# Expert bias in a mixture-of-experts stage: two 128-column transposes and eight products in four row parts of TensorE

## The chip, the cores and the metric

The kernel runs on one core of a Trainium2 chip. The metric is device time in microseconds, the median of several executions. One further execution was recorded by the hardware profiler; all rows below are from it. Matmuls run on TensorE (PE), their weight loads are listed as PEld, VectorE is DVE, ScalarE is ACT, GpSimd is POOL, and SyncE (SP) issues the DMAs.

## What is computed

The program is one transformer-like layer on 8 sequences of 1024 tokens of width 256. A first phase (a selective state-space scan with its projections, then residual and layer norm) gives `x1`. The second phase adds attention with 16 heads of 16 columns and a mixture of 8 experts, and ends in a layer norm:

```
gate = softmax(x @ W_gate + b_gate)                    # 8 values a token
combine = gate at its two largest values, 0 elsewhere
expert_out = einsum("bsd,edf->bsef", x, W_experts) + b_experts
moe_out = einsum("bsef,bse->bsf", expert_out, combine)
return layernorm(x + attn_out + moe_out)
```

The change touches one part of `moe_out`: the bias. Summed over experts it is `combine @ b_experts`, for each tile of 128 tokens a product of a 128x8 with an 8x256 matrix, in fp32.

## The kernel before

The first phase ends at about 1887 us of the span and is not touched. The second one, `attention_phase`, takes the batches b = 0 to 7 one after another: an expert stage (`experts`) and then the heads (`heads`). Each engine has its own instruction list, written by hand, and waits on semaphores; what stands behind a waiting instruction waits too.

In the expert stage the 1024 tokens are 8 tiles t, and a unit u = 4t + e2 is the product of one tile with two experts, six fp16 matmuls of 512 columns (L1419) into one PSUM bank. PSUM has 8 banks; `EBANK[u]` says which one a unit uses, and `used(b, v)` makes TensorE wait until the earlier unit v of the bank was read. DVE weighs the even units and adds them up in `acc` (L1753, L1756, L1764). ACT weighs the odd ones into `scaled` (L1561), and POOL adds those to `x_in` (L1241). DVE's `join` (L1700) adds the two sums of a tile. From unit 13 on, TensorE puts the first scores of the heads in between (L1261), and DVE takes their row maxima (L1628). From batch 1 on DVE also does the layer norm of the batch before (L1674, L1679).

The weights `comb` (128 tokens x 8 tiles x 8 experts) are made by DVE. Behind the units of tile 1 TensorE waits until banks 0 and 1 are free (`used(b, 4)`, `used(b, 5)`) and turns `comb` tile by tile (L1437), ACT copies the result out to `combT` (L1566), and behind the units of tile 2 TensorE forms the eight products with `b_e` (L1445):

```
for q in range(TT):
    mm = pe.transpose(ps[0:E, q // 4, ...], comb[:, q, :], ident[:, :])
...
for q in range(TT):
    mm = pe.matmul(ps[:, q // 2, (q % 2) * H:(q % 2 + 1) * H], combT[:, q * P:(q + 1) * P],
                   b_e[:, :], start=True, stop=True)
```

DVE adds them to the sums in five additions (L1782): three of two tiles, two of one.

The heads start once POOL has done its last addition; there ACT takes the exponentials (L1503), TensorE the scores (L1300, L1261) and the products of the probabilities with v (L1313, four column parts of 32), whose sums it turns back (L1328).

Before the first batch the phase is set up: SP loads weights (L1138 to L1148), POOL clears and fills tiles (L1215 to L1227), DVE and ACT scale the weights. `WEIGHTS` is the count that the engines wait for on the loads.

## Time and profile before

| | us |
|---|---|
| median of 3 runs (3902.52 to 3905.53) | 3902.99 |
| the profiled execution | 3907.31 |
| its span, from the first to the last instruction | 3905.5 |
| busy in the span: PE / DVE / ACT / POOL | 3588.3 / 3426.8 / 2617.0 / 1667.7 |
| mean granted TensorE clock, share of full speed | 0.954 |

In the rows a time is in microseconds from the span's start, and a form as 128x512 is partitions times elements. In a timeline a row gives start, length, engine, line, operation, `out<-in` with the tiles' names, the form and the count of instructions merged in it. In brackets stands how long the engine had been idle before, and which instruction ended that. `combT` is a piece of the tile `probs` and appears under that name. "issue" means that nothing that the profile shows was waited for. An fp32 matmul that isn't a transpose leaves two records.

### The profile page before, as it was taken

Reading aid. Unit: us, or ns where it says so; the run is one execution under the profiler, and the core shown is the slowest. Engines: PE = TensorE matmul, PEld = TensorE weight load, DVE = VectorE, ACT = ScalarE, POOL = GpSimd, SP = SyncE. Lnnn points to the kernel's source line nnn. Section 1 sums busy time; section 2 is a strip of 40 time slices with the busy share of each in tenths; the row PEclk is TensorE's granted clock in tenths of the full one; section 3 lists DMA queues with packets and bytes.
Section 4 is the critical chain, followed back from the end, with each engine's and each line's share of the span. In section 5 each row is a group of like instructions: output and inputs, shape, how many; then the busy total and the mean of one; then the engine's idle time right before and its main releaser. Section 6 shows DMA issues by size and latency. Waiting matters only on the chain.

```text
span 3905.5 us, 121218 instructions
## 1 busy us (share of the span) xinstructions
PE 3588.3 (92%) x52170; PEld 1623.6 (42%) x52170; DVE 3426.8 (88%) x3617; ACT 2617.0 (67%) x3895; POOL 1667.7 (43%) x1054
## 2 busy tenths in 40 slices
PE   5989989899998989898389999999999999999997
PEld 3545455454545545454232423324233242332422
DVE  5898999989999999988689798897988979889796
ACT  4655657665664766655149588595885958869588
POOL 4777778777777777777320110201102011020200
PEclk8999999899999999999699999999999999999999
DMA  3543434444443444443160601506015060240500
GB/s 96 134 116 105 137 100 126 110 132 116 111 137 100 126 121 130 110 102 105 65 86 2 85 26 25 85 2 87 23 27 83 2 87 23 33 78 2 87 12 12
DMA packets 145113, 307.59 MB, mean 79 GB/s; under 512 B 24456, under 2 KB 64016, under 8 KB 144336
## 3 DMA queue, kind: packets, MB, share of 16 engines
q1 hardware_dynamic: 144592, 299.94, 34.0%
q8 instruction: 412, 6.75, 0.7%
q14 instruction: 109, 0.89, 0.1%
HBM read 230.66 MB, written 35.13 MB: 68 GB/s over the span
## 4 chain that ended last, share of the span: by engine, by line
PE 23%; ACT 11%; issue 9%; DVE 7%; POOL 0%; DMA 0%; ACTq 0%; SPq 0%; DVEq 0%; POOLq 0%
ACT probs L1503 9%; PE ps L1313 6%; PE ps L1300 5%; PE ps L1419 4%; DVE neg_max L1628 3%; PE ps L1348 2%; PE ps L1261 2%; PE ps L1328 1%; PE ps L1361 1%; ACT o_sb L1510 1%; PE ps L1445 1%; DVE acc L1764 1%; ACT m_rows L1516 1%; DVE diag_b L1786 1%; DVE x1T L1594 1%
## 5 line engine op out<-in xcount | busy, mean ns | idle before, releaser
L350 POOL TENSOR_TENSOR z<-z,c_rep 128x1024 f32<-128x1024 f32 x512 | 1357.2, 2666 | 457.4 <-DVE z L864 451.7
L1503 ACT ACTIVATE probs<-ps,e_scale 128x512 f32<-128x512 f32 x2048 | 1241.8, 688 | 132.9 <-PE ps L1300 117.8
L864 DVE TENSOR_TENSOR_SCAN z<-dA,ps 128x1024 f32<-128x1024 f32 x512 | 1150.9, 2273 | 130.7 <-PE ps L408 76.2
L1628 DVE TENSOR_REDUCE neg_max<-ps 128x1 f32<-128x1024 f32 x1024 | 1204.2, 1218 | 45.5 <-PE ps L1261 41.1
L705 ACT ACTIVATE dA<-rep,a_rep 128x1024 f32<-128x1024 f32 x512 | 574.3, 1144 | 332.0 <-DVE z L864 327.6
L408 PEld LDWEIGHTS ps<-diag,u_t 64*64 64x64 f32 x32768 | 544.0, 139 | 424.5 <-issue 424.3
L408 PE MATMUL ps<-diag,u_t 64*64 64x64 f32 x32768 | 606.8, 225 | 107.3 <-DVE z L864 84.0
L1300 PE MATMUL ps<-q_st,k_st 50*128 50x512 f16 x2048 | 676.5, 393 | 29.9 <-ACT probs L1503 17.6
L1313 PE MATMUL ps<-probs,v_h 128*32 128x256 f32 x8192 | 658.0, 396 | 0.6 <-ACT o_sb L1510 0.6
L1247 POOL COPY v_h<-v_all 128x80 f32 (+1 forms) x256 | 62.0, 244 | 1283.0 <-PE ps L1313 1283.0
L1261 PE MATMUL ps<-k_st,q_st 48*128 48x512 f16 x2048 | 581.1, 393 | 3.6 <-DVE neg_max L1628 3.5
L427 PE MATMUL ps<-z,eye 128*64 128x512 f32 x2048 | 512.8, 622 | 3.8 <-POOL z L350 2.7
L1241 POOL TENSOR_TENSOR x_in<-x_in,probs 128x256 f32<-128x256 f32 x256 | 191.3, 747 | 417.4 <-ACT probs L1561 405.5
L1419 PE MATMUL ps<-w_e,x1T 128*128 128x512 f16 x1536 | 359.1, 388 | 8.7 <-DVE acc L1764 8.7
L1300 PEld LDWEIGHTS ps<-q_st,k_st 50*128 50x128 f16 x2048 | 159.5, 94 | 467.9 <-ACT probs L1503 240.6
L1313 PEld LDWEIGHTS ps<-probs,v_h 128*32 128x32 f32 x8192 | 168.5, 108 | 361.6 <-issue 181.3
L1561 ACT ACTIVATE probs<-ps,comb_s 128x256 f32<-128x256 f32 x256 | 106.3, 470 | 258.8 <-PE ps L1419 203.9
L427 PEld LDWEIGHTS ps<-z,eye 128*64 128x64 f32 x2048 | 127.4, 139 | 250.8 <-issue 222.9
L1419 PEld LDWEIGHTS ps<-w_e,x1T 128*128 128x128 f16 x1536 | 146.3, 99 | 201.4 <-DVE acc L1764 25.2
L1261 PEld LDWEIGHTS ps<-k_st,q_st 48*128 48x128 f16 x2048 | 133.7, 93 | 60.7 <-issue 25.8
L439 PE MATMUL ps<-w_io,s_res 128*128 128x256 f32 x576 | 139.3, 392 | 1.3 <-DVE s_res L845 1.3
L619 ACT ACTIVATE u_t<-ps 128x1024 f32<-128x1024 f32 x32 | 32.6, 1018 | 146.3 <-PE ps L382 146.3
(189 smaller groups left out, 3283.6 us busy)
## 6 DMA issues: line engine op xcount, KB each, us to landing
c_rep<-c_scratch SPq DMA_DIRECT2D x512, 256.0 KB, 4.0
rep<-delta SPq DMA_DIRECT2D x128, 256.0 KB, 5.0
q_st<-qk_halves SPq DMA_DIRECT2D x192, 128.0 KB, 10.0
k_st<-qk_halves SPq DMA_DIRECT2D x192, 128.0 KB, 10.7
qk_halves<-qk_parts SPq DMA_DIRECT2D x32, 512.0 KB, 11.0
x_nat<-in_x SPq DMA_DIRECT2D x9, 1024.0 KB, 9.7
x_rows<-x_nat SPq DMA_DIRECT2D x9, 1024.0 KB, 6.8
xT<-in_xT SPq DMA_DIRECT2D x8, 1024.0 KB, 7.4
```

Source lines behind the costliest of these rows:

```text
L350: pool.tensor_tensor(z[:, k % ZR, :], z[:, k % ZR, :], c_rep[:, slot, :], ALU.mult).then_inc(s_zc, 1)
L408: mm = pe.matmul(ps[q * QD:(q + 1) * QD, 2 + 2 * (k % 2) + r, i * TB:(i + 1) * TB], u_t[rows, i, m * P + j * QD:m * P + (j + 1) * QD], dia ...
L427: mm = pe.matmul(ps[j * QD:(j + 1) * QD, half, :], eye[:, :], z[:, (grp * QN + j) % ZR, half * HALF:(half + 1) * HALF], start=False, stop= ...
L705: act.activation(dA[:, k % AR, :], rep[:, slot, :], ACT.Exp, scale=a_rep[:, m, j, g:g + 1]).then_inc(s_da, 1)
L864: dve.tensor_tensor_scan(z[:, k % ZR, :], dA[:, k % AR, :], pair(1 + k % 2), 0.0, ALU.mult, ALU.add).then_inc(s_z, 1)
L1241: pool.tensor_tensor(to, to, scaled[:, i % 2, e, :], ALU.add).then_inc(s_pa, 1)
L1261: mm = pe.matmul(ps[:, 2 * (qt % 2) + half, :], head(q_st, half, QR, h, qt * P, P), head(k_st, half, QR, h, half * HALF, HALF), start=True ...
L1300: pe.matmul(ps[:, ring_bank(("probs", h, 2 * kt + half)), :], head(k_st, half, QM, h, kt * P, P), head(q_st, half, QM, h, half * HALF, HAL ...
L1313: mm = pe.matmul(ps[VC * j:VC * (j + 1), 6, 0:n], v_h[:, kt, :], probs[:, kt, j * n:(j + 1) * n], start=(kt == 0), stop=(kt == TT - 1), sk ...
L1419: mm = pe.matmul(ps[:, EBANK[u], :], x1T[:, x, k, t * P:(t + 1) * P], w_e[:, w, k, e2 * 2 * H:(e2 + 1) * 2 * H], start=(i == 0), stop=(i = ...
L1503: act.activation(probs[:, kt, half * HALF:(half + 1) * HALF], ps[:, ring_bank(("probs", h, 2 * kt + half)), :], ACT.Exp, scale=e_scale[:, ...
L1628: dve.tensor_reduce(neg_max[:, qt:qt + 1], pair(qt % 2), AX.X, ALU.max, negate=True).then_inc(s_mx, 1)
```

## The change

`comb` is now laid out with 32 columns a tile (`comb_wide`, 128 x 8 x 32, cleared once on POOL), of which the first 8 hold the weights. So four tiles are 128 columns, and TensorE turns them in one transpose: two instead of eight, both into bank 0. In the result, the weights of tile 4i + j lie in partitions 32j to 32j + 7 and columns 128i to 128i + 127. ACT's copy is 128x256 instead of 8x1024. The table of biases is loaded four times, to partitions 32j to 32j + 7 (three DMAs more, `WEIGHTS` from 16 x 5 to 16 x 8). Each product reads its 8 rows at partition 32j, so four in a row use four different row parts of the array, and they write to four banks, j, at columns 256i. DVE's additions read two neighbouring banks at the same columns instead of 512 columns of one bank. No instruction changes its place in any engine's list; POOL has one more at the start, SP three.

```diff
-        b_e = sb("b_e", [E, H])
+        b_e = sb("b_e", [P, H])
...
-        comb = sb("comb", [P, TT, E])
+        comb_wide = sb("comb", [P, TT, VC])
+        comb = comb_wide[:, :, 0:E]
...
-        combT = probs[0:E, 1, :]
+        combT = probs[:, 1, 0:2 * P]
...
-        WEIGHTS = 16 * 5
+        WEIGHTS = 16 * 8
...
-            for dst, src in ((b_e, d["b_e"]), (b_vg, d["b_vg"].broadcast_to([P, GV]))):
-                sp.dma_start(dst[:, :], src).then_inc(s_w, 16)
+            for j in range(QUARTERS):
+                sp.dma_start(b_e[j * VC:j * VC + E, :], d["b_e"]).then_inc(s_w, 16)
+            sp.dma_start(b_vg[:, :], d["b_vg"].broadcast_to([P, GV])).then_inc(s_w, 16)
...
+            pool.memset(comb_wide[:, :, :], 0.0)
             pool.memset(b_one[:, :], 0.0).then_inc(s_const, 1)
...
-                        for q in range(TT):
-                            mm = pe.transpose(ps[0:E, q // 4, (q % 4) * P:(q % 4 + 1) * P], comb[:, q, :], ident[:, :])
+                        for i in range(2):
+                            mm = pe.transpose(ps[:, 0, i * P:(i + 1) * P],
+                                              comb_wide[:, i * QUARTERS:(i + 1) * QUARTERS, :].rearrange("p j e -> p (j e)"), ident[:, :])
                         mm.then_inc(s_cbt, 1)
...
-                        for q in range(TT):
-                            mm = pe.matmul(ps[:, q // 2, (q % 2) * H:(q % 2 + 1) * H], combT[:, q * P:(q + 1) * P],
-                                           b_e[:, :], start=True, stop=True)
+                        for i in range(2):
+                            for j in range(QUARTERS):
+                                rows = slice(j * VC, j * VC + E)
+                                mm = pe.matmul(ps[:, j, i * H:(i + 1) * H], combT[rows, i * P:(i + 1) * P],
+                                               b_e[rows, :], start=True, stop=True)
                         mm.then_inc(s_eb, 1)
...
-                        act.activation(combT, pair(0)[0:E, :], ACT.Copy).then_inc(s_cbe, 1)
+                        act.activation(combT, ps[:, 0, 0:2 * P], ACT.Copy).then_inc(s_cbe, 1)
...
-                            to = to[:, first:last, :].rearrange("p t h -> p (t h)")
-                            bias = ps[:, first // 2, (first % 2) * H:(first % 2 + last - first) * H]
+                            to = to[:, first:last, :]
+                            i, j = first // QUARTERS, first % QUARTERS
+                            bias = ps[:, j:j + last - first, i * H:(i + 1) * H]
                             dve.tensor_tensor(to, to, bias, ALU.add).then_inc(s_eba, 1)
```

## Rows read from the trace of the kernel before

**Rows 1.** The chain that ended last, 2200 to 2280 us (start, length, what)

```profile
2224.36 3.65 PE ps L1445 x16
...
2233.90 1.21 DVE neg_max L1628
```

**Rows 2.** Waits of DVE, 1968 to 3720 us (total, times, longest)

```profile
DVE x_in L1782 <- PE ps L1445: 24.1, 8, 3.4
```

**Rows 3.** Timeline of DVE, expert stage of batch 1

```profile
2223.11 0.48 DVE L1756 SCALAR_TENSOR_TENSOR acc<-ps,comb_s,acc 128x256 f32<-128x256 f32 x1 [0.65 <-PE ps L1419]
...
2224.69 0.41 DVE L1700 TENSOR_TENSOR acc<-acc,x_in 128x256 f32<-128x256 f32 x1
2228.05 1.62 DVE L1782 TENSOR_TENSOR x_in<-x_in,ps 128x512 f32<-128x512 f32 x3 [2.95 <-PE ps L1445]
...
2232.76 2.35 DVE L1628 TENSOR_REDUCE neg_max<-ps 128x1 f32<-128x1024 f32 x2 [0.65 <-PE ps L1261]
```

**Rows 4.** Timeline of PE, the same stretch

```profile
2218.15 1.03 PE L1437 MATMUL ps<-ident,comb 128*8 128x128 f32 x8 [0.87 <-issue]
2219.02 5.34 PE L1419 MATMUL ps<-w_e,x1T 128*128 128x512 f16 x24
2224.30 3.72 PE L1445 MATMUL ps<-b_e,probs 8*128 8x256 f32 x16
2227.94 4.45 PE L1419 MATMUL ps<-w_e,x1T 128*128 128x512 f16 x12
2232.33 0.60 PE L1261 MATMUL ps<-k_st,q_st 48*128 48x512 f16 x4
```

**Rows 5.** Timelines of DVE and of PE, batch 0, at the bias products

```profile
1988.57 1.62 DVE L1782 TENSOR_TENSOR x_in<-x_in,ps 128x512 f32<-128x512 f32 x3 [3.43 <-PE ps L1445]
...
1988.46 2.76 PE L1419 MATMUL ps<-w_e,x1T 128*128 128x512 f16 x12
```

**Rows 6.** Line 1445 alone (ns), then timeline of PE: products of v, 128-column transposes

```profile
L1445 PE MATMUL ps<-b_e,probs x128: 374/374/478, 1984.8 to 3681.3; 8*128 8x256 f32 x128
...
2169.14 0.64 PE L1313 MATMUL ps<-probs,v_h 128*32 128x256 f32 x8
...
2198.84 2.37 PE L1313 MATMUL ps<-probs,v_h 128*32 128x256 f32 x40
...
2203.84 0.38 PE L1328 MATMUL ps<-ident,o_sb 128*128 128x128 f32 x2
2204.06 2.86 PE L1361 MATMUL ps<-w_vg,x1T 128*128 128x264 f16 x24
```

**Rows 7.** Stretches: window, us, busy us of each engine, then PEclk

```profile
2228.70:2232.10 3.40, 3.40 (x10) 1.07 (x8) 3.37 (x8) 0.00 (x0) 0.00 (x0) 0.50 1.07 125
```

**Rows 8.** Timeline of ACT, batch 1; line 1510 alone (min/median/max ns)

```profile
2219.22 1.02 ACT L1566 ACTIVATE probs<-ps 8x1024 f32<-8x1024 f32 x1 [0.58 <-PE ps L1437]
...
L1510 ACT ACTIVATE o_sb<-ps x128: 382/383/433, 2040.5 to 3884.4; 128x256 f32<-128x256 f32 x128
```

**Rows 9.** Timeline of the set-up, 1884 to 1918 us

```profile
1887.89 0.21 POOL L1215 MEMSET ones<- 128x128 f32 x1 [35.84 <-POOLq L91]
...
1890.88 0.51 SPq L1147 DMA_DIRECT2D b_e<-in_b_e  x1
...
1896.59 20.39 DVE L1786 TENSOR_SCALAR diag_b<-ident,b_qk 128x128 f32<-128x128 f32 x4
1903.05 13.78 POOL L1223 MEMSET k_st<- 32x16384 f16 x1
```

**Rows 10.** Timeline of ACT, first and last exponentials of heads, batches 2 and 3

```profile
2507.91 1.26 ACT L1503 ACTIVATE probs<-ps,e_scale 128x512 f32<-128x512 f32 x2 [1.71 <-POOL x_in L1241]
...
2683.01 1.26 ACT L1503 ACTIVATE probs<-ps,e_scale 128x512 f32<-128x512 f32 x2
...
2751.16 1.26 ACT L1503 ACTIVATE probs<-ps,e_scale 128x512 f32<-128x512 f32 x2 [1.71 <-POOL x_in L1241]
...
2925.45 1.26 ACT L1503 ACTIVATE probs<-ps,e_scale 128x512 f32<-128x512 f32 x2
```

## The prediction

> **What bounds the kernel now.** I read the page first, then the chain that ended last around one batch's expert stage, then the waits of VectorE, then the two engines in order of time. The page's busy shares decide little, for they are averages over stages with different limits, and a matmul's end is modelled. The chain says more. In batch 1 it runs through TensorE up to and through the bias products, and a few microseconds later it passes to VectorE [rows 1], which works almost without a gap until the heads begin. So what ends latest in the expert stage is VectorE's work, as far as TensorE lets it start. The waits say when it does not: 24.1 us in 8 waits for the bias products alone [rows 2].
>
> In batch 1 VectorE stands still three times [rows 3]: 0.65 us for expert unit 10, 2.95 us for the bias products, 0.65 us for the first scores after them. Together 4.25 us. TensorE's side of the same stretch [rows 4]: eight transposes take 0.87 us from their start to the next group's (2218.15 to 2219.02), sixteen records of bias products last 3.72 us (eight fp32 matmuls, two records each). The twelve expert matmuls behind them need 4.45 us, where the same twelve in batch 0 need 2.76 [rows 5]. In batch 0 the wait for the bias is 3.43 us and there is no third one [rows 5]; the other seven then have (24.1 - 3.4) / 7 = 2.95 us each.
>
> **Transposes.** Eight matmuls of 8 columns become two of 128. Two transposes of 128 columns stand in the trace already: they start at 2203.84 and the next matmul at 2204.06 [rows 6], 0.22 us. Saved on TensorE: 0.87 - 0.22 = 0.65 us. Their start does not move: by the code they wait for VectorE's unit 4, and TensorE stood idle 0.87 us before them [rows 4]. The 0.65 us reaches VectorE whole, since unit 10 is what it waits for, for 0.65 us. At the worst the heavier weight load eats 0.1 us; that is the end of the bound.
>
> **Bias products.** Still eight fp32 matmuls of 256 columns and sixteen records, but each set of four stands in four row parts of the array and in four PSUM banks. Before, all sixteen used the same part, one every (3.72 - 0.48) / 15 = 0.216 us (the last one lasts 0.374, the first 0.478 [rows 6]). Row parts of 32 don't occur in this trace. The nearest row is the products of v, four column parts of 32, also fp32 with 256 columns and two records each: one set of eight records lasts 0.64 us and five sets 2.37 us [rows 6], so a set costs (2.37 - 0.64) / 4 = 0.43 us, twice 0.216: four records share one slot. With that the sixteen records take four slots: 3.72 - 12 x 0.216 = 1.13 us. Bounds: 1.13 us if four run together, 1.99 us if two do (eight slots), 3.72 us if none do. I take 1.13, as in the nearest row. The Trainium skill (TensorE: Matmul & The Clock Gate, Part 3, measured speedup) gives 3.07 times for four row parts instead of my 3.29, which would be 1.21 us and 0.6 us less gain over the eight batches; no row here shows row parts of 32.
>
> **Batch 1 with both.** The products start at 2224.30 - 0.65 = 2223.65 and end at 2224.78; VectorE took 0.03 us after the end, so it goes on at 2224.82 instead of 2228.05, 3.23 us earlier. It arrives there at 2225.10 - 0.65 = 2224.45, so 0.37 us of the wait stay.
>
> **The third wait.** VectorE is ready for the scores at 2232.11 - 3.23 = 2228.88 [rows 3]. TensorE begins unit 12 at 2227.94 - 3.23 = 2224.71. What it then needs depends on its clock. The granted clock was 0.50, the lower of the two levels, from 2228.7 to 2232.1, right after 3.7 us in which TensorE used only 8 rows [rows 7]; batch 0 had the same products and kept its speed, 2.76 us for the twelve [rows 5]. With 1.1 us of such products between dense fp16 matmuls I expect no fall. Scores begun at 2232.33 let VectorE go on at 2232.76, 0.43 us later, and at full clock the twelve matmuls take 2.76 us. Then the scores are there at 2224.71 + 2.76 + 0.43 = 2227.90, a microsecond before VectorE, and the third wait goes: 0.65 us. If the clock still falls, the twelve matmuls take 2232.33 - 2227.94 = 4.39 us, the scores come at 2229.53, and 0.65 us of this wait stays.
>
> Sum of a batch from 1 to 7: 3.23 + 0.65 = 3.88 us, seven times 27.2 us. Batch 0 has the first two terms alone: 3.2 us. After that VectorE has no idle time left in the stage that matters, so any further lead of TensorE is worth nothing: it waits for VectorE to free its banks.
>
> **ACT.** Its copy shrinks from 8x1024 at 1.02 us to 128x256, which costs 0.38 us elsewhere [rows 8]. Worth nothing: the copy ended at 2220.24, its reader starts 4 us later. If it were late, it would cost what the products start later.
>
> **DVE's five additions.** Same elements, but two banks are read in one instruction with a step. I take no change. Bound: the first three, two of two tiles and one of one, took 1.62 us, and a single join 0.41 us [rows 3], so a two-tile addition is about 0.6 us and two single ones 0.82. If each fell apart, that is 0.2 us for each of three, 0.65 us a batch, 5 us in all.
>
> **Set-up.** One memset of 128x256 is added on POOL ahead of two of 13.8 us. VectorE's first four small products took 20.39 us and ended at 1916.98, when POOL's last large memset had ended at 1916.83 [rows 9]: it was held up by them. So POOL's order is on the path here, and the new memset costs its own time. 128x128 took 0.21 us, so I take 0.4 us for twice that (0.2 to 0.6). Three more small loads on SP's queue delay the last two by 3 x 0.5 us; POOL needs them at 1917, 25 us after their issue. Nothing; 1.5 us if that cover went.
>
> **Heads.** Their stage is led by ScalarE, starts when POOL has finished the stage before and moves as a whole. Its length depends a little on where low-clock stretches fall: 176.36 us in batch 2, 175.55 us in batch 3 [rows 10]. I take nothing for it and 0.8 us for seven batches as bound, 5.6 us either way.
>
> **Sum.** -27.2 - 3.2 + 0.4 = -30.0 us. The profiled execution took 3907.31 us (span 3905.5) and would take 3877.3; it stands 4.3 us above the median of the three runs, 3902.99 us, and against that the forecast is **3873.0 us**. Its own range: 5.6 us lower through the heads; higher by 4.6 for a clock that falls still, by 5 for the additions, or by 5.6 through the heads, of which hardly more than 8 come together: 3867 to 3881.
>
> **Rivals.**
> Two at a time. The two records of one fp32 matmul stand behind each other in one row part; if the array keeps program order strictly, only neighbours overlap. Then the products take 1.99 us, 0.86 us more in eight batches: -23 us, 3880 us. Against it: the products of v have the same structure and don't show it.
> No overlap at all. Row parts take turns; only the transposes' 0.65 us is left, eight times, less 0.4: about -5 us, 3898 us, within what can be told apart. For it: no row part of 32 with all 128 columns occurs.
> Clock falls anyway, as the transposes of 128 columns or the products still leave a thin stretch: the third wait stays, -30.0 + 7 x 0.65 = -25.5 us, 3877.5 us. For it: in all batches from 1 on it fell before.
> Slower: a drain between row parts. If the array had to be empty before it takes another part, each record would cost its full 0.374 to 0.478 us [rows 6] instead of 0.216: 16 x 0.43 = 6.9 us, 3.2 us more than now. Less the transposes' 0.65, that is 2.5 us in eight batches, +20 us, 3923 us. It decides from 0.26 us a record upwards, where the products lose what the transposes gave. Against it: four column parts started within one slot, 0.43 us for eight records.
> The change is what it says: the two transposes and eight products stand where the eight and eight stood.
>
> **Numbers.** This effect is measurable from about 0.2% (7.8 us). Forecast 0.75; clock falls anyway 0.08; two at a time 0.08; no overlap 0.05; slower 0.04. Range with the first three and their bounds: 3866 to 3881 us. Faster by over 0.2%: 0.91; within: 0.05; slower: 0.04.
>
> **What would show it.** Bias products: sixteen records within about 1.1 us (2.0 and 3.7 for the rivals, 7 for the slower one). VectorE's waits for them together below 5 us instead of 24.1. Transposes to next matmul 0.22 us. Twelve expert matmuls after the products at 2.76 us and a granted clock of 1.00 there. From the first bias addition to the first exponential of the heads 0.65 us less than before in batches 1 to 7. Set-up later by 0.4 us. The forecast is wrong if VectorE shows a new wait between the additions and the heads, or if the heads get longer by over 1 us a batch.

## The result and the profile after

| | before | changed |
|---|---|---|
| median of 6 runs, us | 3905.27 | 3876.31 |
| lowest to highest, us | 3902.52 to 3919.65 | 3873.27 to 3882.33 |
| ratio, 95% interval | | 0.992 (0.9903 to 0.9938) |
| span of the profiled execution, us | 3905.5 | 3880.5 |

The forecast was 3873.0, range 3866 to 3881. The runs of one kernel differ by 9 to 17 us here, and the profiled executions show where most of it lies: in the first phase, which no edit touches. Over the executions below the second phase starts anywhere from 1870.6 to 1890.2 us of the span. So I compare the second phase alone, and split it at three instructions of each batch that stand in the rows: the first expert matmul of TensorE, VectorE's first bias addition, ScalarE's first exponential.

| us | before | changed | forecast of the difference | measured |
|---|---|---|---|---|
| set-up, to the first expert matmul | 80.41 | 80.61 | +0.4 | +0.2 |
| first expert matmul to first bias addition, batch 0 | 20.26 | 17.07 | -3.2 | -3.2 |
| the same, each of batches 1 to 7 | 21.29 | 18.38 | -3.23, seven times | -2.91, seven times |
| first bias addition to first exponential, batches 1 to 7 | 37.9 (38.57 in batch 3) | 38.04 (38.68 and 38.75 in batches 4 and 7) | -0.65, seven times | +1.6 in all |
| first exponential to the next expert matmul, 8 batches | 1466.3 | 1462.0 | 0, bound 5.6 | -4.3 |
| second phase | 2017.6 | 1991.7 | -30.0 | -25.9 |

The timeline of TensorE in batch 1 of the changed kernel, beside [rows 4]:

```profile
2217.29 0.41 PE L1440 MATMUL ps<-ident,comb 128*128 128x128 f32 x2 [0.87 <-issue]
2217.54 5.60 PE L1422 MATMUL ps<-w_e,x1T 128*128 128x512 f16 x24
2223.07 1.15 PE L1451 MATMUL ps<-b_e,probs 8*128 8x256 f32 x16
2224.14 2.76 PE L1422 MATMUL ps<-w_e,x1T 128*128 128x512 f16 x12
2226.93 0.61 PE L1264 MATMUL ps<-k_st,q_st 48*128 48x512 f16 x4
```

The products last 1.15 us for 3.72, and the twelve matmuls behind them 2.76 for 4.45. The transposes still begin after an idle 0.87 us, and the next group starts 0.25 us behind them (before: 0.87). But the 24 matmuls up to the products take 5.53 us from start to start where they took 5.28: TensorE stands 0.25 us more in them, because it now comes too early for a bank that VectorE still reads (unit 11 goes into the bank of unit 8). This is where 0.25 us of the transposes' gain stayed.

The stretches right behind the products, beside [rows 7] (window, us, busy us of each engine, granted clock):

```profile
2223.07:2226.90 3.83, 3.83 (x29) 1.82 (x29) 3.25 (x8) 0.84 (x2) 1.46 (x2) 1.00 1.07 113
2226.90:2230.00 3.10, 3.08 (x17) 1.23 (x16) 3.06 (x5) 0.84 (x2) 1.45 (x2) 1.00 1.04 120
```

The granted clock stays at 1.00, the upper of its two levels. VectorE in the same batch, beside [rows 3]:

```profile
2223.29 0.41 DVE L1706 TENSOR_TENSOR acc<-acc,x_in 128x256 f32<-128x256 f32 x1
2224.28 1.62 DVE L1789 TENSOR_TENSOR x_in<-x_in,ps 128x512 f32<-128x512 f32 x3 [0.58 <-PE ps L1451]
2225.81 1.01 DVE L1789 TENSOR_TENSOR acc<-acc,ps 128x256 f32<-128x256 f32 x2
...
2228.26 2.35 DVE L1634 TENSOR_REDUCE neg_max<-ps 128x1 f32<-128x1024 f32 x2
...
2234.84 0.69 DVE L82 SCALAR_TENSOR_TENSOR ln<-ln 128x8 f32<-128x8 f32 x1
...
2235.68 0.93 DVE L1706 TENSOR_TENSOR acc<-acc,x_in 128x256 f32<-128x256 f32 x1
```

The wait for unit 10 is gone, 0.58 us of the wait for the products is left, the additions take what they took, and the row maxima start with no wait. Its waits over the whole phase, beside [rows 2]:

```profile
DVE x_in L1789 <- PE ps L1451: 4.9, 8, 0.9
```

So far all is as forecast, within 0.35 us a batch. The last two rows of VectorE's timeline are not. In the kernel before the same two instructions stood like this (VectorE, then POOL, same batch):

```profile
2239.41 0.17 DVE L82 SCALAR_TENSOR_TENSOR ln<-ln 128x8 f32<-128x8 f32 x1
...
2239.72 0.42 DVE L1700 TENSOR_TENSOR acc<-acc,x_in 128x256 f32<-128x256 f32 x1
...
2236.66 1.53 POOL L1241 TENSOR_TENSOR x_in<-x_in,probs 128x256 f32<-128x256 f32 x2 [1.62 <-ACT probs L1561]
2239.89 1.64 POOL L1241 TENSOR_TENSOR x_in<-x_in,probs 128x256 f32<-128x256 f32 x2 [1.71 <-ACT probs L1561]
```

and POOL in the changed kernel:

```profile
2234.78 1.54 POOL L1244 TENSOR_TENSOR x_in<-x_in,probs 128x256 f32<-128x256 f32 x2 [1.99 <-ACT probs L1567]
```

Before, the small layer-norm step and the join began in a gap of POOL. Now POOL starts two additions 0.06 us ahead of the step, and the step takes 0.69 us instead of 0.17 and the join 0.93 instead of 0.42, in all seven batches: 1.03 us. This coincidence is a candidate for where the third wait's 0.65 us went. Counted from the first bias addition, VectorE is 0.80 us ahead of the kernel before when the step begins and 0.23 us behind it after the join. Two later joins, 0.54 and 0.78 us long before, take 0.42 and 0.72 now, which leaves the 0.11 us of the table.

The chain that ended last passes from the products to the additions, as in [rows 1], and then stays with VectorE:

```profile
2223.14 1.12 PE ps L1451 x16
2224.49 0.40 issue
2224.88 1.01 DVE x_in L1789 x2
```

Set-up and ACT's copy, beside [rows 8, 9] (POOL, SP's queue, VectorE, ACT):

```profile
1889.08 0.32 POOL L1220 MEMSET comb<- 128x256 f32 x1
...
1892.01 1.44 SPq L1148 DMA_DIRECT2D b_e<-in_b_e  x4
...
1897.78 20.43 DVE L1793 TENSOR_SCALAR diag_b<-ident,b_qk 128x128 f32<-128x128 f32 x4
...
2217.74 0.39 ACT L1572 ACTIVATE probs<-ps 128x256 f32<-128x256 f32 x1
```

The new memset costs its 0.25 us: from the first memset of the phase to the first large one 1.61 us (1.36 before). The whole set-up took 80.35 to 80.74 us in the ten executions with this set-up, and 80.41 and 80.87 in the two with that of before, so the +0.2 of the table isn't told apart from scatter.

Ahead of unit 19 TensorE now stands 1.99 to 2.00 us for VectorE in each of batches 1 to 7 (0.4 us before, 1.2 in batch 3). In five of them the clock stays up, as in batch 1, and in batches 4 and 7 it falls there (TensorE's timeline in batch 1, then in batch 4, then the stretch):

```profile
2237.57 2.76 PE L1422 MATMUL ps<-w_e,x1T 128*128 128x512 f16 x12 [1.99 <-DVE acc L1770]
...
2953.44 4.36 PE L1422 MATMUL ps<-w_e,x1T 128*128 128x512 f16 x12 [2.00 <-DVE acc L1770]
...
2953.30:2956.70 3.40, 3.26 (x8) 1.16 (x9) 3.29 (x6) 0.80 (x4) 0.00 (x0) 0.50 1.06 123
```

The heads' exponentials, first and last of batches 2 and 3, beside [rows 10]:

```profile
2500.62 0.69 ACT L1509 ACTIVATE probs<-ps,e_scale 128x512 f32<-128x512 f32 x1 [1.72 <-POOL x_in L1244]
...
2674.91 1.27 ACT L1509 ACTIVATE probs<-ps,e_scale 128x512 f32<-128x512 f32 x2
...
2739.64 0.69 ACT L1509 ACTIVATE probs<-ps,e_scale 128x512 f32<-128x512 f32 x1 [1.72 <-POOL x_in L1244]
...
2913.47 1.27 ACT L1509 ACTIVATE probs<-ps,e_scale 128x512 f32<-128x512 f32 x2
```

175.56 us (before 176.36) and 175.10 us (before 175.55). The heads begin with a stretch of low clock in both kernels; in batches 1 to 7 it lasts 10.2 us before (6.8 in batch 3) and 6.8 us now. In batch 0 it is the other way round, 6.8 us before and 10.2 now, and that batch's heads are longer now, 183.69 us for 182.53.

### The profile page after: what moved, and what is told of

Its sections match the earlier page's. It is cut to its first block, busy times and chain, and to the rows that moved or that the text cites. A ratio compares the mean times of both kernels' runs of the same rounds, so it can differ in the third digit from the quotient of the medians.

```text
span 3880.5 us, 121126 instructions
## 1 busy us (share of the span) xinstructions
PE 3550.3 (91%) x52122; PEld 1599.7 (41%) x52122; DVE 3431.2 (88%) x3617; ACT 2613.9 (67%) x3895; POOL 1669.2 (43%) x1055
## 4 chain that ended last, share of the span: by engine, by line
PE 20%; ACT 11%; DVE 10%; issue 9%; POOL 0%; DMA 0%; ACTq 0%; SPq 0%; DVEq 0%; POOLq 0%
ACT probs L1509 9%; PE ps L1316 6%; PE ps L1303 5%; DVE neg_max L1634 3%; PE ps L1351 2%; PE ps L1264 2%; PE ps L1422 2%; PE ps L1331 1%; PE ps L1364 1%; DVE acc L1770 1%; ACT o_sb L1516 1%; ACT m_rows L1522 1%; DVE acc L1759 1%; DVE att L1680 1%; DVE diag_b L1793 1%
## 5 line engine op out<-in xcount | busy, mean ns | idle before, releaser
L1509 ACT ACTIVATE probs<-ps,e_scale 128x512 f32<-128x512 f32 x2048 | 1242.5, 690 | 128.5 <-PE ps L1303 113.5
L1264 PEld LDWEIGHTS ps<-k_st,q_st 48*128 48x128 f16 x2048 | 134.5, 93 | 57.0 <-issue 25.9
## 6 DMA issues: line engine op xcount, KB each, us to landing
q_st<-qk_halves SPq DMA_DIRECT2D x192, 128.0 KB, 10.2
```

The costliest lines, as they stand in the source:

```text
L1264: mm = pe.matmul(ps[:, 2 * (qt % 2) + half, :], head(q_st, half, QR, h, qt * P, P), head(k_st, half, QR, h, half * HALF, HALF), start=True ...
L1509: act.activation(probs[:, kt, half * HALF:(half + 1) * HALF], ps[:, ring_bank(("probs", h, 2 * kt + half)), :], ACT.Exp, scale=e_scale[:, ...
```

## The experiments

All times of stages below are of the profiled execution; "products to heads" is from the first bias addition to the first exponential, "heads" from there to the next batch's first expert matmul, summed over eight batches. A ratio is to the kernel before, run beside the one in question.

### The changed kernel again

> The changed kernel once more, beside the next three, so that they can be compared with it on one chip. Same times as before: 3873 to 3882 us. In the profile TensorE's low-clock stretches at the start of the heads are 6.8 us in most batches, where the kernel before had 10.2, if that goes with the new length of a batch and not with one execution.

Measured: median 3879.38 us, ratio 0.9942 (0.9924 to 0.996). Second phase 1991.6 us, products to heads 38.04 us, 38.75 and 38.74 in batches 5 and 7, heads 1462.0. The stages repeat to 0.3 us (most to 0.1); only which batches get the extra low clock differs. The low stretch at the heads' start is 6.8 us in seven of eight batches again. This is the yardstick for the stages below.

### Order of the products

```diff
-                        for i in range(2):
-                            for j in range(QUARTERS):
+                        for j in range(QUARTERS):
+                            for i in range(2):
```

> The changed kernel with its eight bias products in another order: both products of a row part stand next to each other (j outside, i inside), so the four row parts are no longer taken in turn. Work, banks and counts are the same. Theory A (the products overlap because neighbours in the program lie in different row parts, and a record waits for the one before it in its own part): the sixteen records take 2 to 3.5 us instead of 1.15, VectorE waits for them 1.4 to 2.9 us instead of 0.58 in each batch, and the run is 7 to 19 us slower than the changed kernel (3876 us), at 3883 to 3895 us. Theory B (each row part is an independent queue and the order in the program does not matter): 1.15 us, no change in time.

Measured: 3873.82 us, ratio 0.9915 (0.9892 to 0.9938), second phase 1991.5 us. TensorE, batch 1:

```profile
2224.26 1.17 PE L1451 MATMUL ps<-b_e,probs 8*128 8x256 f32 x16
```

1.17 us instead of 1.15, though two products of one row part now follow each other. The rival "two at a time" rested on strict program order between row parts; in this kernel the order doesn't matter.

### Transposes four times

```diff
-                        for i in range(2):
+                        for i in [0, 1] * 4:
```

> The changed kernel with its two transposes issued four times over, which brings back about the 0.87 us of the eight transposes of before (from 0.25) and nothing else. Theory A (in the changed kernel TensorE, 0.65 us earlier after the transposes, stands still 0.28 us for VectorE at unit 11, so only 0.37 us of that gain reaches the bias products): VectorE's wait for the products goes from 0.58 to about 0.95 us, and the run is about 8 x 0.37 = 3 us slower than the changed kernel, 3879 us. Theory B (the whole 0.65 us counts, as the prediction had it): wait 1.2 us, 5 us slower, 3881 us. The clock after the products stays at 1.00 in both; if it falls again, thin work before the products counts too.

Measured: 3878.71 us, ratio 0.9929 (0.9903 to 0.9954). TensorE, then VectorE, batch 1:

```profile
2211.79 1.06 PE L1440 MATMUL ps<-ident,comb 128*128 128x128 f32 x8 [0.87 <-issue]
2212.69 5.34 PE L1422 MATMUL ps<-w_e,x1T 128*128 128x512 f16 x24
...
2216.78 0.49 DVE L1762 SCALAR_TENSOR_TENSOR acc<-ps,comb_s,acc 128x256 f32<-128x256 f32 x1 [0.67 <-PE ps L1422]
...
2219.18 1.62 DVE L1789 TENSOR_TENSOR x_in<-x_in,ps 128x512 f32<-128x512 f32 x3 [0.41 <-PE ps L1451]
```

Eight transposes of 128 columns cost 0.90 us, as the eight of 8 columns did (0.87): it is their number that counts, not their width. TensorE is 0.65 us later, the wait for unit 10 is back at 0.67 us, and yet the first addition comes only 0.40 us later (18.78 for 18.38 us). So fewer transposes are worth 0.40 us a batch at VectorE, not 0.65: the remaining 0.25 us is what TensorE stands for its bank in the changed kernel. And not even the 0.40 us is seen in the total of the profiled execution: its second phase is 1991.3 us, for 1991.7 in the changed kernel. Products to heads is 38.04 in all seven batches, none with extra low clock, though TensorE stands its 2 us there too, and the heads are 1459.8, with 6.8 us of low clock in batch 0 instead of 10.2. By this one execution, then, the transposes' part of the change brought nothing in sum.

### Products over all 128 rows

The biases lie in a block-diagonal table (zeros elsewhere, cleared on POOL in the set-up), so each product uses all 128 rows and the sums are the same. No row part is left for a second product.

```diff
-                                rows = slice(j * VC, j * VC + E)
-                                mm = pe.matmul(ps[:, j, i * H:(i + 1) * H], combT[rows, i * P:(i + 1) * P],
-                                               b_e[rows, :], start=True, stop=True)
+                                mm = pe.matmul(ps[:, j, i * H:(i + 1) * H], combT[:, i * P:(i + 1) * P],
+                                               b_e[:, j, :], start=True, stop=True)
```

> The changed kernel, but each bias product takes all 128 rows: the bias table lies block-diagonally (cleared, 128x4x256), so the same sums come out, with eight products one after the other as before. The transposes stay two. Expected: sixteen records 0.216 us apart, 3.7 us, VectorE waits 3.1 us for them in each batch. Theory A (the clock fell behind the products of before because these used 8 rows only for 3.7 us): the granted clock stays 1.00 after them, the twelve expert matmuls take 2.76 us, and the third wait of VectorE is not there. Theory B (it fell because of what the whole stretch looked like, the wait before the transposes and their 8 columns included, or it goes by time alone): it falls again in most batches and 4.3 us are seen. Total by A: changed kernel plus 8 x 2.57 = 21 us plus 1.2 us for a larger memset in the set-up, 3898 us.

Measured: 3902.3 us, ratio 0.999 (0.9975 to 1.0006), second phase 2015.4 us. TensorE, batch 1, and the stretch behind the products:

```profile
2216.27 3.62 PE L1453 MATMUL ps<-b_e,probs 128*128 128x256 f32 x16
2219.72 2.75 PE L1425 MATMUL ps<-w_e,x1T 128*128 128x512 f16 x12
...
2219.72:2222.50 2.78, 2.75 (x13) 1.08 (x11) 2.58 (x6) 0.00 (x0) 0.00 (x0) 1.00 1.04 119
```

Two things follow. The products last as long as those of 8 rows did [rows 4], but no batch gets the low clock behind them. So their 3.7 us alone did not lower it before. That it was their 8 rows is the likely reading, but not a separate one: the kernel before also had its eight transposes of 8 columns 5.3 us ahead of them, and no run has long 8-row products behind wide transposes. And the third wait is gone in this kernel too, but products to heads takes 38.04 us in batches 1 and 2, not 37.28, and 38.72 to 38.76 in batches 3 to 7. Holding the clock behind the products is by itself worth nothing in this stage. All but 2.2 us of the change's gain in the second phase vanished with the row parts (3.5 us of this is the low clock of batches 3 to 7).

### Products two units earlier

The block of eight products stands behind unit 10 instead of unit 11 (moved as it is).

```diff
+                        if u == 10:
+                            pe.wait_ge(s_cbe, b + 1)
+                            used(b, 6)
+                            used(b, 7)
...
-                    if t == 2:
```

> The changed kernel with the bias products one unit earlier, behind unit 10 instead of unit 11, so that they are ready before VectorE comes to them. What waits behind them is unit 11, for ScalarE, which has time. Expected: VectorE's wait of 0.58 us goes in all batches, 8 x 0.58 = 4.6 us faster than the changed kernel, about 3872 us. Rival: unit 11 comes 1.1 us later, ScalarE and then POOL follow, and join or POOL's next additions collide with VectorE's; then the wait is gone but half or more of it comes back before the heads, 0 to 2 us faster.

Measured: 3871.24 us, ratio 0.9929 (0.991 to 0.9948); second phase 1992.0 us for 1991.7 (the profiled execution's first phase was 17 us shorter, so its span of 3862.6 says nothing). VectorE, then POOL, batch 1:

```profile
2204.18 1.61 DVE L1788 TENSOR_TENSOR x_in<-x_in,ps 128x512 f32<-128x512 f32 x3
2205.70 1.01 DVE L1788 TENSOR_TENSOR acc<-acc,ps 128x256 f32<-128x256 f32 x2
2206.63 1.10 DVE L1679 TENSOR_TENSOR att<-att,acc 128x512 f32<-128x512 f32 x1
...
2205.65 1.53 POOL L1244 TENSOR_TENSOR x_in<-x_in,probs 128x256 f32<-128x256 f32 x2 [2.24 <-ACT probs L1566]
```

The wait for the products is zero in every batch and the additions come 0.66 us earlier (17.72 us), but products to heads grows to 38.45, and 39.17 where the clock falls, in five of seven batches. A layer-norm addition behind them takes 1.10 us for 0.69: it reads two operands from SBUF and runs beside POOL. The bias additions ahead of it, with one operand in PSUM, run beside POOL as well and take the 1.01 us that they always took. Again what a wait gives, 0.66 us, is mostly taken back within the same stage, 0.41 us: the rival of the expectation.

### POOL's additions away, first try

POOL's two additions of unit 15 are left out (`i` counts the odd units from 0).

```diff
+                        if i == 7:
+                            pool.sem_inc(s_pa, 1)
+                        else:
```

> The changed kernel without POOL's two additions for unit 15 (their contribution is left out of the sum of tile 3), to see what they do to VectorE. In the changed kernel the small layer-norm step at line 82 takes 0.69 us and the join after it 0.93 us while these additions run; before, at another time, they took 0.17 and 0.42. Theory A (VectorE's operations on SBUF alone stand still while POOL works on its 128x256 additions): line 82 takes 0.17 us in all seven batches, the join 0.42, and from the first bias addition to the heads 37.0 us pass instead of 38.04. Theory B (these steps are slow for another reason, ScalarE's table load or the bank reads): no change in them. Total by A: 7 us faster than the changed kernel.

Measured: 3878.57 us in one run, second phase 1991.4 us; the layer-norm step at 0.69, the join at 0.93, products to heads 38.03 (38.67 and 38.70 in batches 4 and 6). A miss of the experiment, not of the theory: at the time of the step POOL runs the additions of unit 17, not of unit 15.

### POOL's additions away, second try

Now those of unit 17 are left out.

```diff
+                        if i == 8:
+                            pool.sem_inc(s_pa, 1)
+                        else:
```

> The changed kernel with the two additions of POOL for unit 17 (the ninth odd unit) left out, so that 1/16 of the odd units' sums is missing; the semaphore counts stay. My last attempt took unit 15's away, which was the wrong one: at 2231.28 us of that span POOL still ran an addition of 1.5 us while VectorE's layer-norm step started at 2231.34. Theory A (what gave the third wait's 0.65 us back is VectorE's small steps starting together with that addition): the step takes 0.17 us again instead of 0.69, the join behind it 0.42 instead of 0.93, and from the first bias addition to the first exponential batches 1 to 7 take 37.0 to 37.3 us instead of 38.04. Theory B (the steps are long for another reason, their place behind the previous instruction or a change of operand): 0.69 and 0.93 stay, 38.04 as well.

Measured: 3877.54 us in one run. VectorE, batch 1:

```profile
2230.29 0.17 DVE L82 SCALAR_TENSOR_TENSOR ln<-ln 128x8 f32<-128x8 f32 x1
...
2230.60 0.43 DVE L1709 TENSOR_TENSOR acc<-acc,x_in 128x256 f32<-128x256 f32 x1
```

Both have their old durations, and products to heads takes 37.01 us (37.36 in one batch). With the same edit at unit 15 nothing moved, so it is this addition. This settles where the third wait's 0.65 us went. With 1.03 us less, the stage is 0.9 us shorter than in the kernel before. Yet the second phase is 1989.8 us, not 7 us shorter: the heads take 1468.7 us instead of 1462.0.

### The join first

```diff
-                    if t == 3 and late is not None:
-                        ln_stats(late)
                     if t:
                         join(b, t - 1)
+                    if t == 3 and late is not None:
+                        ln_stats(late)
```

> The changed kernel with the join of tile 2 ahead of the six small layer-norm steps instead of behind them. Nothing is left out. If VectorE loses about 1 us there because five of these operations meet POOL's additions (Theory A), the order decides which are hit: the join now starts 0.9 us earlier, mostly before the additions, and takes 0.42 to 0.7 us; the layer-norm steps may be hit instead, one by one. 0 to 0.5 us a batch, 0 to 3.5 us faster. If the loss has nothing to do with timing against POOL, the sum of these seven operations stays 2.1 us.

Measured: 3875.12 us, ratio 0.993 (0.9914 to 0.9947), second phase 1990.1 us. VectorE, batch 1:

```profile
2234.40 0.41 DVE L1706 TENSOR_TENSOR acc<-acc,x_in 128x256 f32<-128x256 f32 x1
...
2234.89 0.17 DVE L80 TENSOR_TENSOR ln<-stats 128x8 f32<-128x8 f32 x1
2235.09 0.58 DVE L82 SCALAR_TENSOR_TENSOR ln<-ln 128x8 f32<-128x8 f32 x1
```

and POOL:

```profile
2234.83 1.64 POOL L1244 TENSOR_TENSOR x_in<-x_in,probs 128x256 f32<-128x256 f32 x2 [1.99 <-ACT probs L1567]
```

Products to heads is 37.29 us in all seven batches, 0.75 less, where at most 0.5 was expected, with nothing left out of the computation. The heads gave most of it back, 1467.2 us. That is the same pattern as in the run without unit 17's additions, and the clock shows it: the low stretch at the heads' start is 10.2 us again in six of eight batches (the changed kernel: in one).

### All rows, and the pause filled

The kernel with products over all rows, plus:

```diff
+                            if u == 18:
+                                for i in range(8):
+                                    pe.matmul(ps[:, 7, :], x1T[:, 0, 0, 0:P], w_e[:, 0, 0, 0:2 * H], start=True, stop=True)
```

> The kernel with bias products over all 128 rows (block-diagonal biases), one after another, and eight extra fp16 matmuls of 512 columns on TensorE behind the scores that follow unit 18, into bank 7, whose result nobody reads. They fill the place where TensorE stood about 2 us for VectorE, ahead of unit 19. Theory A (that pause is what the low clock 13 us behind the products comes from): no stretch at 0.50 between the products and the end of the stage in any batch, where the kernel without the extra matmuls had one of 3.4 us in batches 3 to 7; first bias addition to first exponential 38.04 us in all seven batches, none at 38.7; products still 3.62 us and the wait for them 2.92 us. Theory B (the low stretch belongs to what happened earlier, in the products or before): it stays in four or five batches. Theory C (the extra matmuls themselves delay VectorE): 38.04 grows by up to 1 us everywhere.

Measured: 3894.88 us in one run, second phase 2012.5 us (2015.4 without the extra matmuls). TensorE, batch 1:

```profile
2232.54 1.90 PE L1437 MATMUL ps<-w_e,x1T 128*128 128x512 f16 x8
2234.61 2.76 PE L1425 MATMUL ps<-w_e,x1T 128*128 128x512 f16 x12 [0.16 <-DVE acc L1775]
```

The pause ahead of unit 19 shrinks from 1.99 to 0.16 us, and no batch has low clock between the products and the heads; products to heads is 38.03 to 38.05 in batches 1 to 7 (five of them took 38.7 without). So Theory A: it was TensorE's pause for VectorE that brought these stretches, at 0.65 to 0.7 us each, in this one execution. The changed kernel has the same pause in front of those of batches 4 and 7; there I read the cause from this run. The pause doesn't bring a stretch each time: of the seven pauses of 2 us in an execution, five were followed by one with all rows and with the products two units earlier, two in the changed kernel, and none with the transposes four times. Pauses of 1.0 to 1.3 us, as in the runs with the join first and without unit 17's additions, were followed by none. What decides among the pauses of 2 us is open. Batch 0 got 0.8 us longer.

### Join first, clock held at the start of the heads

The join-first kernel with the same eight matmuls behind unit 18 and eight in the first head. `fill(bank, n, cols)` issues n such matmuls into a bank, of 512 columns where `cols` isn't given:

```diff
+                        if h == 0 and not before and kt == 1 and half == 0:
+                            fill(6, 8)
```

> The changed kernel with the join ahead of the layer-norm steps (37.29 us instead of 38.04 from the first bias addition to the first exponential, already seen) and with two groups of eight extra fp16 matmuls of 512 columns each that nobody reads: behind the scores after unit 18 into bank 7, and in the first head of every batch, second key tile, first half, into bank 6. They take away TensorE's thin places at the end of the stage and the start of the heads. Theory A (the stage's gain was given back because the low-clock stretch at the heads' start grew from 6.8 to 10.2 us): that stretch is gone or under 4 us, first exponential to the next batch's experts sums to at most 1460 us over eight batches (1467.2 without the extra matmuls, 1462.0 in the changed kernel), second phase 1983 to 1987 us instead of 1991.6, median about 3868 to 3872 us against 3877. Theory B (the low stretch doesn't cost the heads anything, they are led by ScalarE): the stretch goes but the sum stays at 1462 to 1467. Theory C (the extra matmuls of 1.7 us delay the scores that ScalarE waits for): sum above 1467, time 3880 us or more.

Measured: 3871.35 us, ratio 0.9911 (0.9894 to 0.9927), second phase 1981.3 us, heads 1454.8. Batches 1, 4 and 6 have no low stretch at the heads' start, and each takes 180.35 us. Those with 3.4 us of it take 181.8 to 181.9, the one with 6.8 us 183.5. Theory A, but for one batch with 6.8 us of it, and a price: a low stretch at the start of the heads costs 1.4 to 3.1 us, since ScalarE waits there for scores. Products to heads is 37.68: the extra matmuls behind unit 18 delay it by 0.39 us.

### More of it in the first head

Without those behind unit 18, and one of 256 columns behind each later pair of scores of the first head up to key tile 3:

```diff
+                        elif h == 0 and not before and 1 <= kt < LAG:
+                            fill(6, 1, H)
```

> The changed kernel with the join ahead of the layer-norm steps and the eight extra matmuls in every batch's first head, without those behind unit 18, and with one extra matmul of 256 columns behind each pair of scores from key tile 1 (second half) to 3 of that head, where TensorE waits about 0.19 us of every 0.58 us for ScalarE. The extra results are read by nobody. Two questions that the stages keep apart. First, the ones behind unit 18 delayed the first exponential (37.68 us against 37.29 from the first bias addition): 37.29 is expected in batches 1 to 7. Second, the heads. Theory A (the pauses of 0.19 us are what let the clock fall in the batches that still fell): no low stretch at any heads' start, 180.35 us from first exponential to next experts in batches 1 to 6, as in the three batches without one; second phase about 1973 us instead of 1981.3, median 3860 to 3865. Theory B (what decides falls earlier, or the ones behind unit 18 were needed here too): stretches of 3.4 to 10.2 us in most batches, 181.8 to 183.5 us. Theory C (they delay ScalarE by 0.02 to 0.1 us each): 180.5 to 181.0 us where no clock fell.

Measured: **3853.76 us** (3841.71 to 3855.18), ratio **0.9871** (0.9852 to 0.989), second phase 1969.0 us. The first 15 us of batch 2's heads, granted clock in the third last column, for the kernel before:

```profile
2507.91:2522.91 15.00, 14.09 (x95) 3.02 (x95) 11.58 (x17) 12.72 (x23) 0.77 (x3) 0.66 0.22 71
```

for the changed one:

```profile
2500.62:2515.62 15.00, 13.53 (x99) 3.11 (x99) 12.35 (x18) 13.44 (x24) 0.78 (x3) 0.77 0.22 71
```

for join first:

```profile
2499.49:2514.49 15.00, 14.10 (x96) 3.16 (x96) 11.88 (x18) 12.97 (x23) 0.77 (x3) 0.66 0.21 71
```

and for this one:

```profile
2488.42:2503.42 15.00, 14.51 (x129) 4.38 (x127) 13.84 (x20) 14.94 (x27) 1.00 (x4) 1.00 0.21 71
```

0.66, 0.77, 0.66, 1.00: the heads' sum goes the same way, 1466.3, 1462.0, 1467.2, 1446.2 us. In 15 us ScalarE does 14.94 us of work instead of 12.7 to 13.4. Its idle time ahead of the exponentials of the whole execution, put down to TensorE's scores, is (us, times)

```profile
  PE ps L1303: 101.4, 176
```

where it was 117.8 before, 113.5 in the changed kernel and 118.4 with the join first. There is no low stretch at any heads' start, products to heads is 37.28 to 37.30, and heads takes 180.3 to 180.8 in batches 0 to 6. That is Theory A, with more than the 1973 us that it gave. It computes the same and beats both kernels: its second phase is 22.7 us shorter than the changed kernel's, 6.6 of it between the products and the heads and 15.8 in the heads, and the two intervals of the ratios don't overlap.

### The extra matmuls on the kernel before

> The kernel before with the eight extra matmuls in the first head alone. Theory A (the clock at the heads' start has nothing to do with the bias, and what is won there comes on top of the change): heads in sum 1455 to 1462 us instead of 1469, second phase 2005 to 2010 us instead of 2017.6, the waits for the bias products unchanged at 24 us, ratio 0.995 to 0.997. Theory B (without the shorter bias products TensorE comes to the heads with the low clock anyway): sum within 2 us of 1469, no gain that can be told.

(1469 in this expectation is a slip; the kernel before has 1466.3.) Measured: 3901.09 us, ratio 0.9997 (0.9986 to 1.0009), second phase 2015.1 us. The heads won 6.5 us (1459.8) as Theory A has it, and batches 0, 1 and 3 took 180.35. But the stages in front lost 3.5 us and the set-up 0.5: in batches 2 and 4 the clock now fell already during the long 8-row products. TensorE, batch 2:

```profile
2452.06 4.29 PE L1452 MATMUL ps<-b_e,probs 8*128 8x256 f32 x16
2456.28 5.30 PE L1426 MATMUL ps<-w_e,x1T 128*128 128x512 f16 x12
```

4.29 and 5.30 us for 3.72 and 4.45, and VectorE's wait for the products is 3.5 us in these two batches. Theory A was right on the heads and wrong that nothing else moves: its ratio of 0.995 to 0.997 was missed. Of the heads' 6.5 us, 2.5 us are left in the second phase. The further matmuls of the run before were not tried on this kernel.

This run has one more thing to say on the third wait. In its batches 0, 5 and 7 the clock stayed up behind the long products. Batches 5 and 7 then took 38.04 and 38.03 us from products to heads, as the changed kernel does, and not 37.28. So in the kernel before, too, losing that wait gained nothing.

## Why the prediction was right, and where a step of it was not

- **Bias products: right.** 1.13 us forecast, 1.15 measured, where it was 3.72: a factor of 3.2. The neighbour that I priced it by, the column parts of the products of v, was a good one. Turning the loop over showed that the order is no condition. With all rows the gain in the second phase falls to 2.2 us.
- **VectorE 3.23 us earlier: 2.91.** "The 0.65 us reaches VectorE whole" failed. TensorE is limited by banks as well as by its own work: 0.25 us of the lead is spent waiting for one. The run with fourfold transposes put 0.40 us on what fewer of them give. The lead is 0.32 us short of the forecast, 7 x 0.32 = 2.2 us, and the wait that is left is 0.58 us, not 0.37.
- **The clock behind the products stays up: right.** With 128 rows 3.6 us of the same products don't lower it either, so the time alone is not the reason; that the 8 rows are stays the likely reading. The long 8-row products don't lower it each time: in seven of eight batches before, in five of eight in the run with extra matmuls on that kernel.
- **"The third wait goes: 0.65 us": the wait went, the time didn't.** This is the step that failed, seven times 0.65 us, 4.6 us. I took a removed wait for a gain without asking what VectorE's later instructions would run into. They ran into POOL's additions for 1.03 us. Two runs show it from both sides: without that unit's additions 37.01 us, with the join moved ahead 37.29, against 38.04. One of the prediction's signs, 0.65 us less from products to heads, thus failed, while its warning, a new wait of VectorE, didn't appear: the time went into longer instructions, which no list of waits shows.
- **"After that VectorE has no idle time left": right and not enough.** TensorE's 2 us pause for VectorE now and then brought the low clock: 1.3 us in two batches. The run with the pause filled shows it, in one execution of the kernel with all rows.
- **Heads: -4.3 us, where I took nothing** and 5.6 us as bound. The low stretch at their start fell from 10.2 to 6.8 us in six of eight batches. Holding the clock there brought 180.35 us a batch, so the length of the heads follows this stretch and not ScalarE's own work. That the -4.3 us are this too is read from the batches, for the most part: batch 3, with 6.8 us in both kernels, got 0.46 us shorter all the same. Why the changed kernel gets 6.8 us there and join first 10.2 us is not settled; the extra matmuls show what the stretch costs, not what picks its length.
- **ACT, additions: right.** Set-up: 0.25 us for the new memset, forecast 0.4.

Together: -30.0 was forecast; 2.2 us stayed at the banks, 6.2 us behind the additions (4.6 of the third wait, and 1.6 since the stage is even a little longer than before, part of it low clock), the heads gave 4.3 and the set-up 0.2: -25.9 up to rounding. Between the medians of the runs it was -29.0, with the first phase's scatter in it. The forecast came within 3.3 us of the median, and 2.3 us of these come from the kernel before, whose median over six runs is 3905.27 us where it was 3902.99 over three. But that is partly luck: 8.4 us lost and 4.5 us won that weren't forecast had opposite signs, and the scatter of the first phase gave another 3 us. The rival "clock falls anyway" had -25.5 us for the second phase and would have come nearest to the measured -25.9, though the clock didn't fall behind the products and the third wait went.

## What to carry to other kernels

Small fp32 products of few rows belong in separate row parts and banks: four at a time take one's time, in any order. A wait that disappears is a gain only if the instructions behind it don't land beside another engine's that hold them up, as POOL's additions did here for 1.03 us, so lay the timelines of both engines over each other with the shift in. And where a stage is led by another engine that needs TensorE's results, look at TensorE's granted clock at the stage's start; a few microseconds of useless dense matmuls in its pauses, together with one join moved, brought another 22.7 us of the second phase here, where the change had brought 25.9.

## What the runs showed of the hardware

- A step of VectorE that reads two operands from SBUF can be held by a POOL addition, even a small one: 128x8 took 0.69 us instead of 0.17 when it started 0.06 us behind one, and 0.58 when 0.26 us behind. In both cases it ended when POOL's addition of 0.7 to 0.8 us did. The Trainium skill (GPSIMD Engine Reference, 1. Specifications) has POOL contend with VectorE's instructions of two SBUF inputs for the shared interfaces; the trace agrees, and adds that a step of 0.17 us can wait three times its length. The bias additions, with one operand in PSUM, were not held (1.01 us beside POOL and without it). It isn't certain from the starts who is held: in the join-first run the step at line 80, also of two operands from SBUF, started 0.06 us behind POOL and took its 0.17 us, and there POOL's addition took 0.82 us instead of 0.73.
- Eight fp32 products of 8 rows in four row parts: sixteen records of 0.374 to 0.478 us in 1.15 us, where one row part took 3.72 us.
- The granted clock fell to 0.50 within 1.2 us of the end of 3.7 us of 8-row matmuls in seven of eight batches (with extra matmuls in the first head, during or behind them in five of eight). Behind 3.6 us of 128-row ones and behind 1.15 us of 8-row ones it did so in none.
- A transpose of 8 columns costs TensorE as much as one of 128, 0.11 us.
- Extra matmuls cost little where ScalarE leads: the first head's took nothing that shows (180.35 us in the batches with a full clock, the least that any kernel had).
